# When the |w| scan of the second weight matrix loads its tiles: one group ahead on ScalarE's queue

## The reference, cut to what matters

```python
def layer(x, w_qkv, w_o, W_fc, ln_w, ln_b, W_proj):      # x: 16 x 2048 x 1024
    # attention with one head: softmax over the axis of heads (size 1), so each weight is 1
    h = layernorm(x)
    q, k, v = split(h @ w_qkv.T, 3)
    att = softmax(q @ k.T * SCALE, axis=1)                # all ones
    x = x + (att @ v) @ w_o.T
    # feed-forward with ternary weights
    h = layernorm(x)
    h = gelu(h @ absmean(W_fc).T)                         # 4096 wide
    h = layernorm(h) * ln_w + ln_b
    return x + h @ absmean(W_proj).T

def absmean(W):
    gamma = mean(abs(W)) + 1e-6
    return sign(W / gamma) * minimum(round(abs(W / gamma)), 1.0)
```

## Time and profile before

| what | us |
| --- | --- |
| median of 2 runs (3699.34 to 3702.81) | 3701.07 |
| the profiled execution's own time | 3697.26 |
| its span on the slowest core, core 3 | 3695.7 |
| spans of the 8 cores | 3680.2 to 3695.7 |
| TensorE busy on core 3 | 2896.2 (78%) |
| DVE busy | 2238.5 (61%) |
| ACT busy | 869.8 (24%) |

### The profile page before, as it was taken

One profiled execution on the slowest core, in us unless ns is written; L12 is line 12 of the kernel. 1 busy time (PEld: TensorE's weight loads), 2 busy tenths in 40 slices (PEclk: granted clock), 3 DMA queues, 4 the chain that ended last, 5 costly groups with the idle time before them and its releaser, 6 DMA issues.

```text
span 3695.7 us, 66863 instructions; the slowest of 8 cores (3680.2 to 3695.7 us)
## 1 busy us (share of the span) xinstructions
PE 2896.2 (78%) x22170; PEld 1959.3 (53%) x22170; DVE 2238.5 (61%) x5462; ACT 869.8 (24%) x2133; POOL 71.6 (2%) x148
## 2 busy tenths in 40 slices
PE   0001250898989898989898989898989898989896
PEld 0001240565656565656565656565656565656564
DVE  5556775656566656666665656565656565656544
ACT  1113500322222222222222222222222222222211
POOL 0000022000000000000000000000000000000000
PEclk9999999999999999999999999999999999999998
DMA  3335823000000000000000000000000000000000
GB/s 126 103 125 195 276 90 103 12 13 12 13 13 13 13 13 13 13 13 13 13 13 13 13 13 13 13 13 13 10 15 7 18 7 18 7 18 1 12 1 12
DMA packets 38403, 130.26 MB, mean 35 GB/s; under 512 B 7216, under 2 KB 7344, under 8 KB 38064
## 3 DMA queue, kind: packets, MB, share of 16 engines
q1 hardware_dynamic: 18864, 67.22, 5.6%
q10 hardware_dynamic: 9216, 33.56, 2.8%
q0 software_dynamic: 9984, 25.20, 1.9%
HBM read 109.15 MB, written 16.78 MB: 34 GB/s over the span
## 4 chain that ended last, share of the span: by engine, by line
PE 71%; DVE 11%; DMA 8%; issue 3%; ACT 3%; DVEq 2%; POOL 1%; ACTq 1%; SPq 0%; POOLq 0%
PE proj_ps L229 35%; PE fc_ps L682 34%; DMA x1s<-wpT 6%; DVE cols L51 3%; DVE x1s L51 3%; DVEq L50 2%; DMA xs<-wfcT 2%; DVE bnp L51 1%; PE trp_ps L663 1%; DVE gps_t L51 1%; ACT qp_t L51 1%; ACTq L50 1%; DVE rrq L51 1%; ACT qf_t L51 1%; POOL l2t_t L349 1%
## 5 line engine op out<-in xcount | busy, mean ns | idle before, releaser
L229 PE MATMUL proj_ps<-qp_t,gps_t 128*128 128x512 bf16 x6144 | 1431.4, 383 | 172.0 <-DVE gps_t L51 171.8
L682 PE MATMUL fc_ps<-l2t_t,qf_t 128*128 128x256 bf16 x12288 | 1445.9, 275 | 0.7 <-ACT l2t_t L51 0.7
L682 PEld LDWEIGHTS fc_ps<-l2t_t,qf_t 128*128 128x128 bf16 x12288 | 1199.9, 99 | 180.3 <-issue 1.4
L229 PEld LDWEIGHTS proj_ps<-qp_t,gps_t 128*128 128x128 bf16 x6144 | 603.5, 99 | 811.4 <-issue 209.0
L51 ACT ACTIVATE g<-fc_ps 128x256 f32<-128x256 f32 x512 | 197.2, 385 | 2027.7 <-PE fc_ps L682 1878.2
L51 DVE TENSOR_TENSOR S<-S,g 128x256 f32<-128x256 f32 x496 | 211.0, 425 | 759.4 <-ACT g L51 756.2
L51 DVE SCALAR_TENSOR_TENSOR rrq<-g,lnw_c,gps_t 128x256 f32<-128x256 f32 x512 | 248.3, 485 | 38.7 <-issue 0.6
L51 ACT ACTIVATE l2t_t<-trp_ps 128x128 bf16<-128x128 f32 x768 | 213.2, 278 | 133.2 <-PE trp_ps L663 73.4
L516 PE MATMUL trp_ps<-identb,l2t_t 128*128 128x128 bf16 x48 | 6.6, 299 | 302.8 <-DVE l2t_t L51 301.5
L51 DVE TENSOR_TENSOR gps_t<-rrq,gps_t 128x256 bf16<-128x256 f32 x512 | 217.5, 425 | 40.7 <-issue 3.5
L51 DVE TENSOR_TENSOR S<-S,gsq 128x256 f32<-128x256 f32 x496 | 210.9, 425 | 42.0 <-issue 6.1
(11 more groups left out here) (127 smaller groups left out, 1376.8 us busy)
## 6 DMA issues: line engine op xcount, KB each, us to landing
xs<-x SPq DMA_DIRECT2D x64, 512.0 KB, 4.1
x1s<-wpT ACTq DMA_DIRECT2D x64, 512.0 KB, 4.0
xs<-wfcT SPq DMA_DIRECT2D x64, 512.0 KB, 4.8
out<-x1s POOLq DMA_DIRECT2D x32, 512.0 KB, 2.9
x1s<-wvT POOLq DMA_DIRECT2D x8, 512.0 KB, 6.4
x1s<-woT POOLq DMA_DIRECT2D x8, 512.0 KB, 7.6
l2t_t<-gps_t POOLq DMA_DIRECT2D x96, 0.2 KB, 1.6
xs<-ident SPq DMA_DIRECT2D x1, 64.0 KB, 6.2
```

What stands on the lines that cost most here:

```text
L229: last = tensor.matmul(out=proj_ps[tg][:, 512 * hh:512 * hh + 512], lhsT=gps[jj % 2][s][:, 128 * tg:128 * tg + 128], rhs=qp[jj][:, 512 * h ...
L682: last = tensor.matmul(out=fc_ps[j % 2][:], lhsT=qf[d][:, 128 * j:128 * j + 128], rhs=l2t[i % 2][s][d][:], start=(s == 0 and d == 0), stop ...
```

## The change

ACT issues the `wpT` loads of groups 0 and 1 right after its first table load, before the loop. In the loop, where it issued the load of group gr, it now issues that of group gr + 2 into the same buffer, and waits first for `B_scanp` at gr + 1, that is, for the scan of group gr itself, which reads this buffer. Groups 30 and 31 issue none. The number of loads and all else is the same; DVE's, SP's, POOL's and TensorE's queues are unchanged.

```diff
--- before.py
+++ after.py
@@ -386,6 +386,10 @@
         def _(scalar):
             scalar = _AutoDrain(scalar)
             scalar.preload_act_table(AF.Sqrt)
+            if do_b:
+                for gr0 in range(2):
+                    scalar.dma_start(out=x1s[2 + gr0 % 2][:],
+                                     in_=wpTg[gr0, :, :]).then_inc(B_x1p[gr0 % 2], 16)
             for gr in range(NG):
                 scalar.wait_ge(A_rc, gr + 1)
                 scalar.activation(out=r2c[0][:], in_=rcc[0][:], func=AF.Sqrt)
@@ -396,11 +400,10 @@
                 scalar.activation(out=ATT1[:], in_=xs[gr % 2][:], func=AF.Identity,
                                   bias=biasc[0][:], scale=r2c[0][:])
                 scalar.inc(A_ln1s, 1)
-                if do_b:
-                    if gr >= 2:
-                        scalar.wait_ge(B_scanp, gr - 1)
+                if do_b and gr + 2 < NG:
+                    scalar.wait_ge(B_scanp, gr + 1)
                     scalar.dma_start(out=x1s[2 + gr % 2][:],
-                                     in_=wpTg[gr, :, :]).then_inc(B_x1p[gr % 2], 16)
+                                     in_=wpTg[gr + 2, :, :]).then_inc(B_x1p[gr % 2], 16)
                 if gr % 16 == 15:
                     b = gr // 16
                     accdead = U if b == 0 else ATT0
```

## The result

| | before | after |
| --- | --- | --- |
| median, us | 3698.36 (6 runs, 3695.66 to 3705.34) | 3664.05 (7 runs, 3661.33 to 3669.46) |
| ratio | | 0.9905, 95% interval 0.9893 to 0.9917 |
| the profiled execution's own time | 3697.26 | 3669.56 |
| spans of its 8 cores | 3680.2 to 3695.7 | 3652.4 to 3668.0 |

The change gains 34.3 us by the medians, 0.93% (0.95% by the ratio), clear of the measurement's own uncertainty and well under 2%. The prediction was 3660.5 us, in a range of 3650 to 3673.

What follows compares the result with a forecast made beforehand. TensorE bounds the untouched main loop; before it, DVE's wpT waits are on the path. 43.5 - 2.6 - 2.3 = 38.6 us gain gives 3658.7 us from the profiled execution, 3662.5 from the median; predicted 3660.5, range 3650 to 3673.

Steps and rivals of the forecast that it cites:

- The wait on the path: First phase: DVE's 32 waits on the wpT load, 43.5 us, end; gain 40.9 us on core 3.
- A group of 7.3 us: First phase: without the load wait, a group takes 7.3 us instead of 8.62.
- The start: Start of the kernel: two early wpT loads delay the identity, by 0 to 4.6 us; 2.3 us taken.
- a rule: Start: engines go round queues packet by packet, so the identity pays for one wpT load at most, 2.3 us.
- The row's reading: Start: the identity pays for all that is in flight, 1.05 MB at 230 GB/s, 4.6 us.
- ACT's queue: First phase: the issue's added wait on ACT costs nothing, since ACT is free 1.8 us before it is wanted.
- The rival with 10 us: First phase: issue and wait on ACT hold up the square root, 10 us, giving 3670.5 us; chance 0.05.
- The `x` load: First phase: stays hidden, 10.3 us of room; rival: it takes the wait's place, 3701 us, chance 0.03.
- The rival that the loads don't land ahead: First phase: the load is late again, needing a landing over 13 us; no gain, 3701 us; chance 0.01.
- The prediction's rival, by which it takes back the gain and more (55 us): Quantization phase: aligned cores slow 22 wpT loads, 55 us, 3715.5 us; chance 0.05 for giving back wholly or in good part.
- The prediction's allowance of 5 us either way for this phase: Next phase, before the main loop: range allowance of 5 us, half the 10 us by which cores differ there.
- the footing: Whole kernel: gain taken from the profiled execution (3697.3 us) and the median (3701.1 us), giving 3658.7 and 3662.5 us.

Runs made afterwards that it cites:

- e6: Kernel before with its wpT load issued one step earlier, ahead of the activation of its own group; ratio 0.9941 to the kernel before.
- e2: Changed kernel with both loads ahead of the loop waiting for the first rows of x; ratio 0.9888 to the kernel before.
- e5: Changed kernel with only group 0's load at the start, group 1's waiting for the first rows of x; 3663.8 us in one run.
- e8: Changed kernel with loads one group ahead, no wait on the same group's scan, one start load after x's first rows; ratio 0.9884 to the kernel before.
- e10: On top of e3: first x loads don't wait for the identity, and DVE scans the weight tile before the add; ratio 0.9748 to the kernel before.
- e9: Kernel before run again for its profile, no edit; 3706.59 us.
- e1: Changed kernel run again, no edit; ratio 0.9905 to the kernel before.
- e11: Kernel before with DVE's scan of the weight tile moved ahead of the add that waits for ACT; ratio 1.0113 to the kernel before.
- e3: On top of e2, GpSimd's first wvT loads also wait, for the first activation; 3659.19 us in one run.
- e7: Changed kernel with an add of a zero tile to itself on VectorE in each first-phase group; ratio 1.0019 to the kernel before.

## Why the prediction was right

**The wait on the path.** Predicted: 43.5 us go, less 0.08 us for each of 32 gaps, 40.9 us on core 3. There the stretch from the first statistics to the last scan fell from 299.6 - 13.14 = 286.5 us to 262.1 - 15.47 = 246.6 us, by 39.8. The 1.1 us between them are in part in the waits on ACT, which are 0.8 us longer in sum (25.1 to 25.5, 16.0 to 16.4). e6 shows the rate by a smaller dose: 23 to 27 us of the wait gone, 22 us gained (14 to 30). A group of 7.3 us was forecast and 7.35 came.

**The start.** Taken as 2.3 us between 0 and 4.6, a middle between a rule and a row. The identity is 3.0 us later and the first statistics 3.2 us in the mean over the cores; on core 3, 2.8 and 2.3. e2 shows that the early loads cause it and e5 that it goes with the bytes. The row's reading ("it pays for all that is in flight") was the right one, but its price of 4.6 us was too dear: 0.40 of the 1.05 MB passed before 4.4 us, in slices that had been almost idle (0.53 MB there against 0.13 on core 3). As an estimate from these rows, the other 0.65 MB at 230 GB/s take 2.8 us, which is what core 3 shows. That 2.3 us, the middle, came near was luck: neither of the two readings gives it, and the 2.3 us of the rule for one load is not what one load costs (1.5 us).

**ACT's queue.** Costed at nothing for its 1.8 us of room: e8, without that wait, is no shorter (246.5 us from the first statistics to the last scan, 246.2 in e2, which has it). The rival with 10 us falls.

**The `x` load** never shows as a releaser after the first rows, not even in e10 with 5.86 us per group. The rival that the loads don't land ahead falls with the waits of zero.

**The second phase.** The prediction's rival, by which it takes back the gain and more (55 us), falls by the total. That it takes back 3 to 5 us is not borne out by e9 either. In the mean over the cores the runs on e1's chip went from 3694.0 to 3658.6 us, by 35.4, and the last scan, by two profiles of each kernel, from 298.8 to 262.1 us, by 36.7. What is left for the second phase, 1 us or so, is within the scatter, and these runs don't tell it from nothing. The prediction's allowance of 5 us either way for this phase was about what single executions show.

**The number.** 3664.05 against 3660.5; as a gain, 34.3 us by the medians against 38.6 in the sum. About 0.9 us of this is the dearer start (3.2 against 2.3), and 0.8 the waits on ACT, which were taken as unchanged. Where the rest lies, some 2 to 3 us, no run separates. It is no more than the scatter of the footing: I took the profiled execution and the median of two runs as the kernel's time and a core's drift from one profile. That profile was of a short execution, while waits and second phase scatter by several us from one to the next. The waits that go were 43.5 us on its slowest core, and up to 47.4 us in e9.

## What to carry to other kernels

A load issued beside the work that it should hide behind is late by the difference of the two, here about 1.3 us in each of 32 groups. Half of that lead took away half of the wait (e6), and with two buffers a whole group of lead costs nothing (e8). Once the data is there early, look at what its consumer can now be moved into: filling the other engine's wait (e10) gave more than the lead itself, and without the lead (e11) the same move loses. Here loads that were wanted later, on either of two other queues, held up a small one that everything waited for; it is worth holding them back until it has landed. Before a few us between two stages are explained, take a second profile of the kernel before.

## What the runs showed of the hardware that was not expected

A load of 64 KB with only two of 16 KB ahead of it landed 2.8 us after its issue in the mean over the cores (e3), and with 1.05 MB of loads from another queue beside it, 5.7 us (the kernel before). Each further 0.52 MB put on a third queue just ahead of it added 1.5 us, the second as much as the first (e5: 7.2 us; after: 8.7 us). And in the one profile with an added add on VectorE in the first phase (e7), the main loop, 370 us later, took 2989.7 us in the mean over the cores; the means of the twelve other profiles lie between 2984.9 and 2986.6. Whether the add is the cause, and what would carry over, wasn't found.
